# Attention row sums copied out of PSUM by the scalar engine, and the normalisation steps issued one key block later

## What is computed

```python
attn = jnp.einsum('bhqd,bhkd->bhqk', query_states, key_states) * SOFTMAX_SCALE
attn = jax.nn.softmax(attn.astype(jnp.float32), axis=-1).astype(query_states.dtype)
out = jnp.einsum('bhqk,bhkd->bhqd', attn, value_states)
out = out.transpose(0, 2, 1, 3).reshape(b, s, NH * V_DIM)
return out @ wo

x = x + _layernorm(_L0_attn_ref(_layernorm(x), ...))
x = x + _layernorm(_L0_ffn_ref(_layernorm(x), ...))
```

## Time and profile before

| what | us |
|---|---|
| median of the runs (2 runs) | 828.08 |
| range of the runs | 827.42 to 828.73 |
| the profiled execution | 827.81 |
| span of its slowest core (core 4) | 826.3 |
| spans of the eight cores | 818.4 to 826.3 |
| mean granted clock of PE, core 4 | 0.871 of full |

### The profile page before, as it was taken

One profiled execution on the slowest core, in us unless ns is written; L12 is line 12 of the kernel. 1 busy time (PEld: TensorE's weight loads), 2 busy tenths in 40 slices (PEclk: granted clock), 3 DMA queues, 4 the chain that ended last, 5 costly groups with the idle time before them and its releaser, 6 DMA issues.

```text
span 826.3 us, 9694 instructions; the slowest of 8 cores (818.4 to 826.3 us)
## 1 busy us (share of the span) xinstructions
PE 599.8 (73%) x3012; PEld 284.6 (34%) x3056; DVE 431.9 (52%) x710; ACT 388.6 (47%) x569; POOL 40.8 (5%) x67
## 2 busy tenths in 40 slices
PE   0356666649888888888888886864652549999991
PEld 0245454403333333333333332321222534444440
DVE  1555656345555555555555552474886761534543
ACT  0577777627777777777777775021213210000000
POOL 2700000010000000000000000210000000000000
PEclk9985556559999999999999999886985869999996
DMA  8934441079800000000000000896444001234231
GB/s 176 243 99 108 113 143 52 0 98 170 142 1 1 1 0 1 1 1 0 1 1 1 0 1 1 185 209 230 166 153 187 18 3 25 102 153 152 102 150 55
DMA packets 15586, 67.03 MB, mean 81 GB/s; under 512 B 5800, under 2 KB 5808, under 8 KB 9392
## 3 DMA queue, kind: packets, MB, share of 16 engines
q0 software_dynamic: 10624, 32.85, 18.0%
q1 hardware_dynamic: 4912, 33.56, 12.8%
HBM read 65.70 MB, written 16.78 MB: 100 GB/s over the span
## 4 chain that ended last, share of the span: by engine, by line
PE 46%; DVE 25%; DMA 10%; issue 8%; ACT 8%; DVEq 1%; POOL 0%; ACTq 0%; another core or an unknown queue 0%; POOLq 0%; SPq 0%
PE psF L1028 14%; PE psO L627 6%; PE psO L630 5%; PE psS L641 5%; PE psS L644 4%; DMA xmid<-xre 2%; DVE den_r L674 2%; DMA Wt<-wt 2%; PE psC L389 2%; DMA wqkva_b<-wqkva 2%; DMA ktwt_b<-ktwt 2%; DVE woL L614 2%; DVE recB L611 2%; DVE st6b L753 2%; DVE st6c L805 2%
## 5 line engine op out<-in xcount | busy, mean ns | idle before, releaser
L649 ACT ACTIVATE eS<-psS 128x1024 bf16<-128x1024 f32 x256 | 247.1, 1022 | 96.7 <-PE psS L644 96.2
L1028 PE MATMUL psF<-Wt,lnT 128*128 128x512 bf16 x500 | 113.3, 385 | 1.7 <-DVE xaT L947 1.0
L641 PE MATMUL psS<-QX,cT 128*128 128x512 bf16 x241 | 94.4, 392 | 10.5 <-ACT eS L649 8.9
L627 PE MATMUL psO<-eS,V 128*65 128x512 bf16 x256 | 97.5, 381 | 5.1 <-DVE woL L614 4.7
L644 PE MATMUL psS<-QX,cT 128*128 128x512 bf16 x249 | 97.1, 390 | 4.0 <-ACT eS L649 3.7
L630 PE MATMUL psO<-eS,V 128*65 128x512 bf16 x256 | 97.2, 380 | 0.0
L784 PE MATMUL psW<-wo_b,woL 128*128 128x512 bf16 x251 | 65.8, 425 | 35.4 <-DVE xre L797 31.6
L758 ACT ACTIVATE rstdb<-mvb,eps_b 128x1 f32<-128x1 f32 x16 | 4.7, 294 | 156.9 <-DVE mvb L756 156.9
L363 PE MATMUL psP<-ident_b,lnb 128*128 128x128 bf16 x256 | 30.8, 287 | 61.8 <-ACT slab L371 31.5
L1028 PEld LDWEIGHTS psF<-Wt,lnT 128*128 128x128 bf16 x512 | 50.0, 99 | 64.3 <-issue 7.1
L753 DVE BATCH_NORM_STATS2 st6b<-psF 128x6 f32<-128x512 f32 x32 | 19.9, 685 | 69.2 <-PE psF L1044 69.2
(11 more groups left out here) (124 smaller groups left out, 699.3 us busy)
## 6 DMA issues: line engine op xcount, KB each, us to landing
xtmp<-x_full SPq DMA_DIRECT2D x16, 1024.0 KB, 6.0
Wt<-wt POOLq DMA_DIRECT2D x16, 512.0 KB, 20.5
xre<-x_full SPq DMA_DIRECT2D x8, 1024.0 KB, 5.9
xmid<-xre POOLq DMA_DIRECT2D x8, 1024.0 KB, 4.7
xre<-xmid SPq DMA_DIRECT2D x8, 1024.0 KB, 4.7
out<-xre POOLq DMA_DIRECT2D x8, 1024.0 KB, 4.1
wo_b<-wo POOLq DMA_DIRECT2D x1, 4096.0 KB, 31.2
wqkva_b<-wqkva POOLq DMA_DIRECT2D x1, 768.0 KB, 18.1
```

The source lines that it names most:

```text
L627: e.matmul(psO[0:65, 0:512], Vsb[kt][:, h * 65:(h + 1) * 65], eS[kb][:, 0:512], start=(kt == 0), stop=(kt == RT_F - 1), skip_group_check=True)
L641: e.matmul(psS[ks][:, 0:512], cT[:, kt * 128:(kt + 1) * 128], QX[hb][:, 0:512], start=True, stop=True)
L649: lambda e, kb=kb, ks=ks: e.activation(eS[kb][:, :], psS[ks][:, 0:1024], AF.Exp, scale=SCALE))
L1028: inst = e.matmul(psF[qb][:, c * 512:(c + 1) * 512], lnT2[q][:, t * 128:(t + 1) * 128], Wt_sb[t][:, c * 512:(c + 1) * 512], start=(t == 0) ...
```

## The change

Two edits. The copy `den_r` becomes an Identity activation on ACT, at the same place in the program. And the three remaining steps of the tail are issued at `kt` = 1, 2, 3 in place of 0, 1, 2. No instruction is added or taken away, and all sizes stay as they are.

```diff
                     if h > 0:
-                        if kt == 0:
+                        if kt == 1:
                             head_den(h - 1)
-                        elif kt == 1:
+                        elif kt == 2:
                             head_tail_a(h - 1)
-                        elif kt == 2:
+                        elif kt == 3:
                             head_tail_b(h - 1)
                     if kt >= 5:
                         emit_av(kt - 5)
...
-                P.run("dve", [B("psO")], [B("denr")],
-                      lambda e: e.tensor_copy(den_r[0:1, :], psO[64:65, 0:1024]))
+                P.run("act", [B("psO")], [B("denr")],
+                      lambda e: e.activation(den_r[0:1, :], psO[64:65, 0:1024],
+                                             AF.Identity))
             head_den(NH - 1)
             head_tail_a(NH - 1)
             head_tail_b(NH - 1)
```

## The result

| | before | changed |
|---|---|---|
| median, us | 827.75 (8 runs) | 853.79 (9 runs) |
| the profiled execution, us | 827.81 | 853.57 |
| span of its slowest core, us | 826.3 (core 4) | 852.0 (core 7) |
| ratio to before | 1 | 1.0316 (95% interval 1.0304 to 1.0328) |

The changed kernel is 3.2% slower, 26 us. Executions in which one half of the chip was disturbed are left out of this ratio and of all that follow; the median of nine has one of them in it and is 853.77 without it. Rows of the changed kernel are of core 7 where nothing else is said.

The account below looks back on a forecast made before the run. The prediction took the start of AV(0), behind the tail at each head boundary, to bound the kernel. It summed 827.8 + 8.0 (order) + 13.0 (clock) = 848.8, said 849 us, range 833 to 857.

Parts of the forecast that it names:

- slower: Whole kernel: time above 844.6 us, beyond the 2% within which no change can be told; chance 0.58.
- The bound: Head boundary: when AV(0) may start sets the head; the tail takes 6.31 us of 20.64.
- The order: Head boundary: copy ahead of exp(0) and later steps bring AV(0) 0.55 us later, 8.0 us in all.
- exp(0) starts at +0.93: ACT at the boundary: behind the copy, exp(0) starts 0.93 us after `den_r` starts, 0.50 later than before.
- The clock: PE at the boundaries: thinner work makes the clock fall in seven heads, 1.99 us each; 13.0 us added.
- the two holes: PE at the boundary: end of S(1) to S(4), then to AV(0) at +6.86; twice as many as before.
- the one long case on core 2: Kernel before, head beginning at 260.00: clock at 0.50 into the busy part, 23.25 us against 21.26, 1.99 lost.
- Rival 1: Whole kernel: the order costs its 8 us, the clock stays as it is; 835.8 us, chance 0.32.
- Rival 2: Head boundary: exp(0) does not wait for the copy, tail 0.20 us earlier at 16 places; 824.6 us, chance 0.05.
- Rival 3: ACT: Identity and Exp need different tables, two loads at each copy, 41 us; 877 us, chance 0.02.
- Rival 4: PE: the clock falls in all 15 heads; 864.8 us, chance 0.05.
- same: Whole kernel: within 2% of the kernel before, 811.5 to 844.6 us; chance 0.40.

Follow-up runs that it names:

- the run with both copies: Changed kernel with the real `den_r` back on DVE and an unread copy of the same length on ACT: 850.59 us, ratio 1.0288.
- the filled kernels: Unread matmuls added at each of 15 boundaries: nine against the changed kernel, 835.69 us, ratio 1.0106; six against the kernel before, ratio 1.0019.
- the early hole filled: Changed kernel with four unread matmuls a boundary, between S(1) and S(3), the hole ahead of AV(0) left open: 847.07 us, ratio 1.0241.
- the late one filled: Changed kernel with five unread matmuls a boundary, ahead of AV(0), the holes between S(1) and S(4) left open: 839.14 us, ratio 1.0149.

## Why the prediction was right

The forecast was 849 us, the range 833 to 857, and the time is 853.8; slower had the larger chance. Its points, one by one:

**The bound.** AV(0) of each head waits for `woL`, and what AV(0) loses the head loses. Held: full-clock heads have 14.31 to 14.33 us behind AV(0) in the kernel before, the changed one, the one with the steps moved and the one with the copy moved (20.64 - 6.31, 21.38 - 7.07, 20.77 - 6.45, 20.46 - 6.14).

**The order, mis-sized.** Forecast 0.55 a boundary and 8.0 in all; measured 0.75 (+7.07 against +6.31) and 10.0. The step that was mis-sized is "exp(0) starts at +0.93": I had put the copy in the rhythm of back-to-back exps. It starts when the copy has ended, at +1.04, and everything in that chain moves with it, so that S(3) is at +3.13 in place of +3.03. L605 then comes 0.31 behind the second matmul of S(3) where I had 0.22, and from L605 to AV(0) it is 3.42 in place of 3.39. The copy's own length, 1.02, was right. The chain copy, exp(0), S(2) was right, and the run with both copies shows it by itself.

**The clock, right in kind.** Forecast seven falls of 1.99, 13.0 net; measured nine of 1.85 on core 7, 16.0 net. That the two holes do it was argued from the kernel before alone; the filled kernels show it now, for both holes and for each alone. The length of a fall, taken from the one long case on core 2, was within a tenth. The number of falls had no ground but the bounds, and that it came out between them is luck. Both terms were too small, by 2 and by 3 us, which is why the time is 5 us above the figure, and still inside the range.

**Rival 1** (order alone) has in the filled kernel its own measurement: 835.7, for 835.8 worked out. The agreement is partly luck, since the order was sized 2 us too low and the falls of the kernel before had been left in. **Rival 2** is close to what the copy alone gives, 3.4 us where it was put at 3.2, though by another way: exp(0) does wait for the copy, each boundary gains 0.17, and what is needed is L596 ahead of S(2). **Rival 3**: the changed kernel has one table load in all, as before, and exp(0) starts 0.02 behind the copy's end. **Rival 4**: nine heads, not all 15.

Three smaller slips of the prediction change nothing in its sum. The groups of PE instructions in the tail are three (L583, L596, L605), not four. The chances of its cases add up to 1.00 without the 0.02 for what was not seen, so that "same" is 0.42 by them. And "two of 15" is core 4 alone; core 2 has two short falls and the long one.

## What to carry to other kernels

A move to another engine has to be checked in that engine's queue: a 1 us copy on an idle ACT was worth 3 us saved with the steps of the tail early, and some 21 lost with them late (832.2 to 853.8), depending on what was waiting for the exp that it delayed. Where PE's clock already falls now and then, a delay that thins its work out can cost more than its length: here 10 us of order brought 16 us of clock. Matmuls that nobody reads, put into the holes, separate the two in one run, as long as AV(0) does not have to wait for them. And an accumulator that blocks the next round is best copied out whole: here the copy of 65 rows cost what the copy of one did, and with AV closer to its exp and the steps later it gave 3.2%.

## What had not been expected of the hardware

- An exp behind another exp starts 0.93 after it, although each takes 1.02. Behind the Identity copy of one PSUM row it starts at 1.04, after its end; behind the same copy from a bf16 row in SBUF (1.06 long) at 0.97. What makes the difference was not tried.
- The falls repeat in a pattern. With the early hole filled they come in every second head almost without exception (22.96, 21.38, 22.96, 21.38 and so on), with the late one filled in every third (22.11, 21.38, 21.38).
- A small matmul of the tail behind an S pair (L596, L605) starts 0.30 and 0.31 after the pair's second matmul, where the second starts 0.22 after the first.
